# Moving the experts' up product from VectorE to ScalarE and GpSimd in a Mamba and mixture-of-experts kernel

## The reference, cut to what matters

```python
x = x + layernorm(mamba(layernorm(x)))        # x: 8 sequences x 1024 tokens x 256
x = x + layernorm(moe(layernorm(x)))

# inside mamba: 512 channels x 16 states
dA  = exp(dt[..., None] * A)
dBx = dt[..., None] * B[:, :, None, :] * xc[..., None]
h   = dA_t * h + dBx_t                        # a scan over the tokens
y_t = sum over states of h * C_t
y   = (y + xc * D) * silu(z) @ out_proj

# inside moe: 16 experts, 4 chosen per token, combine holds 0 for the others
g = einsum('th,eih->tei', x, gate_proj)
u = einsum('th,eih->tei', x, up_proj)
act = silu(g) * u
y = einsum('teh,te->th', einsum('tei,ehi->teh', act, down_proj), combine)
```

## Time and profile before

| what | value |
|---|---|
| median of 3 runs | 2711.35 us (2710.67 to 2711.61) |
| profiled execution | 2710.63 us, of which the span from first to last instruction 2708.8 us |
| VectorE busy | 2437.7 us, 90% of the span |
| TensorE busy | 2403.0 us, 89% |
| ScalarE busy | 1632.9 us, 60% |
| GpSimd busy | 1509.4 us, 56% |

### The profile page before, as it was taken

How to read it: one execution, slowest core, us unless ns; L and a number is a source line. 1 busy time by engine, 2 the same in 40 slices (tenths; PEclk the granted TensorE clock), 3 DMA queues, 4 the chain that set the end, 5 groups by cost and what they waited for, 6 DMA issues and landing times.

```text
span 2708.8 us, 27117 instructions
## 1 busy us (share of the span) xinstructions
PE 2403.0 (89%) x8416; PEld 1179.6 (44%) x8416; DVE 2437.7 (90%) x3236; ACT 1632.9 (60%) x3312; POOL 1509.4 (56%) x546
## 2 busy tenths in 40 slices
PE   5556898999989899998989999898999989898988
PEld 2112354544535454443545445353544535443554
DVE  3999999999999999999999999999999999999642
ACT  5566566566766656666665666666566666644331
POOL 0555555556665555665555566555656655565521
PEclk9778999999999999999999999999999999999999
DMA  4342434435353353535344353533535343352321
GB/s 157 139 146 81 156 109 133 158 115 163 120 161 110 130 163 115 163 120 158 113 131 163 100 177 120 161 110 127 167 109 169 120 154 109 127 163 84 86 59 60
DMA packets 174923, 352.38 MB, mean 130 GB/s; under 512 B 16283, under 2 KB 81596, under 8 KB 166332
## 3 DMA queue, kind: packets, MB, share of 16 engines
q1 hardware_dynamic: 164700, 334.93, 37.1%
q0 software_dynamic: 10080, 15.73, 3.6%
HBM read 291.35 MB, written 51.38 MB: 127 GB/s over the span
## 4 chain that ended last, share of the span: by engine, by line
DVE 59%; issue 18%; ACT 14%; PE 8%; DMA 1%; POOL 0%; DVEq 0%; SPq 0%; ACTq 0%; POOLq 0%
DVE hs L1019 27%; DVE hs L1005 13%; DVE th L1129 5%; DVE th L1134 5%; PE Gp L479 2%; ACT DX L604 2%; PE Up L487 2%; PE MY L497 2%; DVE XC L972 2%; ACT dA L586 1%; ACT L586 1%; ACT XC L657 1%; ACT SZ L662 1%; ACT my L765 1%; ACT DX L727 1%
## 5 line engine op out<-in xcount | busy, mean ns | idle before, releaser
L897 POOL TENSOR_TENSOR hs<-hs,Cb 128x2048 f32<-128x2048 f32 x256 | 1170.9, 4574 | 165.9 <-DVE hs L1005 165.9
L586 ACT ACTIVATE dA<-dtr,A 128x512 f32<-128x512 f32 x1024 | 701.8, 690 | 830.7 <-DVE hs L1019 829.7
L877 POOL TENSOR_TENSOR th<-th,cmb 128x512 f32<-128x512 f32 x256 | 338.2, 1326 | 818.1 <-DVE hs L1005 712.6
L1019 DVE TENSOR_TENSOR_SCAN hs<-dA,carry,hs 128x512 f32<-128x512 f32 x512 | 628.2, 1264 | 19.9 <-ACT dA L586 19.6
L1019 DVE TENSOR_TENSOR_SCAN hs<-dA,hs 128x512 f32<-128x512 f32 x512 | 595.9, 1203 | 30.7 <-ACT dA L586 30.2
L479 PE MATMUL Gp<-x2T,Wgu 128*128 128x512 f32 x1024 | 528.1, 640 | 106.1 <-DVE th L1129 105.9
L1005 DVE TENSOR_TENSOR hs<-dxr,Bb 128x2048 f32<-128x2048 f32 x256 | 602.7, 2354 | 7.7 <-DMA dxr<-dx_d 7.5
L487 PE MATMUL Up<-x2T,Wgu 128*128 128x512 f32 x1024 | 492.6, 604 | 0.0
L497 PE MATMUL MY<-Wdn,th 128*128 128x256 f32 x2048 | 485.7, 381 | 0.8 <-POOL th L877 0.8
L497 PEld LDWEIGHTS MY<-Wdn,th 128*128 128x128 f32 x2048 | 383.3, 190 | 136.7 <-issue 91.9
L479 PEld LDWEIGHTS Gp<-x2T,Wgu 128*128 128x128 f32 x1024 | 180.8, 195 | 439.1 <-issue 246.3
(11 more groups left out here) (165 smaller groups left out, 1860.5 us busy)
## 6 DMA issues: line engine op xcount, KB each, us to landing
dtr<-dt_d SPq DMA_DIRECT2D x64, 1024.0 KB, 5.6
dxr<-dx_d SPq DMA_DIRECT2D x128, 512.0 KB, 7.3
cmb<-cm_d SPq DMA_DIRECT2D x256, 256.0 KB, 3.7
Wdn<-in_w_dn SPq DMA_DIRECT2D x256, 128.0 KB, 3.6
Bb<-bc_d SPq DMA_DIRECT2D x64, 256.0 KB, 3.1
Cb<-bc_d SPq DMA_DIRECT2D x64, 256.0 KB, 4.1
dt_d<-XB SPq DMA_DIRECT2D x15, 1024.0 KB, 4.3
dx_d<-DX SPq DMA_DIRECT2D x15, 1024.0 KB, 5.9
```

The lines of the kernel that those rows point to most:

```text
L586: act.activation(dA[h % 2][:, :], dtr[:, M % 2, beta, :], ACT.Exp, scale=A[:, k:k + 1]).then_inc(s_dA, 1)
L877: pool.tensor_tensor(th[:, q % NTH, :], th[:, q % NTH, :], cmb[:, q % 2, :], ALU.mult).then_inc(m_a, 1)
L897: pool.tensor_tensor(hs[:, G % NH, :, :], hs[:, G % NH, :, :], Cb[:, s, :].unsqueeze(1).broadcast_to([P, NBETA, CH]), ALU.mult).then_inc(s ...
L1019: dve.tensor_tensor_scan(hv, dA[h % 2][:, :], hv, first, ALU.mult, ALU.add).then_inc(s_h, 1)
```

## The change

- ScalarE gets `keep_up`: it copies the up product from PSUM (Up) to a new SBUF buffer Ub. VectorE's `expert_up` is gone.
- GpSimd's `weigh` becomes two multiplications, Ub = Ub * cmb and th = th * Ub, and runs one group earlier (experts of G-1 in place of G-2).
- TensorE's up matmuls wait for `keep_up` in place of `expert_up`; `load_cm` waits for the first of the two multiplications two experts earlier.
- ScalarE's other work is moved between groups: the four z evictions and their fills (z0 to g = 4, z1 to g = 6 and 7, z2 and z3 to g = 9, ahead of the fill for dt), `p_x2` from the end of g = 6 to the middle of g = 7, `e_norm` from g = 7 to 8, `f_silu_z` from g = 12 to 10. `p_sums2` is removed: the mean of x1 is that of x, which is kept in x_nm.
- Some small buffers shrink or are shared (ln1, Ebias, z_s, to_y inside hs), and to_y comes by a DMA of its own.

```diff
-FILLS = ['b2', 'k2', 'r0', 'r1', 'b3', 'k3', 'z0', 'xp', 'x0', 'x1', 'rt', 'db', 'z1', 'ct', 'z2', 'z3', 'xT0', 'xT1', 'b0', 'b1']
+FILLS = ['b2', 'k2', 'r0', 'r1', 'b3', 'z0', 'k3', 'z1', 'xp', 'x0', 'x1', 'rt', 'z2', 'z3', 'db', 'ct', 'xT0', 'xT1', 'b0', 'b1']
...
+        Ub = sb('Ub', [P, CH])
...
                 if q % NE == 0:
                     sp.wait_ge(st_cm, 16 * (q // NE + 1))
                 if q >= 2:
-                    sp.wait_ge(m_a, q - 1)
+                    sp.wait_ge(m_w, q - 1)
                 sp.dma_start(cmb[:, q % 2, :], cm_d[q].partition_broadcast(P)).then_inc(ld_cm[q % 2], 16)
             def load_wd(q):
                 if q >= NWD:
...
             def up(q):
                 c, e = divmod(q, NE)
                 if q >= 1:
-                    pe.wait_ge(m_w, q)
+                    pe.wait_ge(m_us, q)
                 for k in range(KM):
                     mm = pe.matmul(Up[:, :], Wgu[:, k, e, DE:2 * DE], x2T[:, c % 2, k, :], start=k == 0, stop=k == KM - 1)
                 mm.then_inc(m_u, 1)
...
                 if now:
                     gate(now[0])
                     up(now[0])
-                if F and g in (0, 4, 6, 11):
-                    f_in(p, {0: 'b2', 4: 'b3', 6: 'z0', 11: 'z3'}[g])
+                if F and g in (0, 4, 6, 9):
+                    f_in(p, {0: 'b2', 4: 'b3', 6: 'z1', 9: 'z2'}[g])
                 if F and g in (1, 5):
                     f_conv(p, PE_CONV[g // 4])
                 if F and g == 7:
                     f_x(p)
-                if F and g == 9:
-                    f_dt(p)
                 if R_ and g in (2, 3):
                     p_out(p, g - 2)
                 if R_ and g == 8:
...
                     p_turn(p, 0)
                 if R_ and g == 8:
                     p_route(p)
-                if F and g in (9, 10):
-                    f_in(p, f'z{g - 8}')
+                if F and g == 4:
+                    f_in(p, 'z0')
+                if F and g == 9:
+                    f_in(p, 'z3')
+                    f_dt(p)
                 if in_e(p) and g == 13:
                     e_turn(p, 1)
                 if len(now) == 2:
...
                     act.wait_ge(m_d, q - NTH + 1)
                 act.activation(th[:, q % NTH, :], Gp[:, :], ACT.Tanh, scale=0.5).then_inc(m_th, 1)
 
-            def sums(x, s, to=None):
+            def keep_up(q):
+                act.wait_ge(m_u, q + 1)
+                if q >= 1:
+                    act.wait_ge(m_a, q)
+                act.activation(Ub[:, :], Up[:, :], ACT.Copy).then_inc(m_us, 1)
+
+            def sums(x, s):
                 for b in range(TB):
-                    ins = act.activation(to[b] if to else x[:, b, :], x[:, b, :], ACT.Copy, accum_out=s[:, 0, b:b + 1])
+                    ins = act.activation(x[:, b, :], x[:, b, :], ACT.Copy, accum_out=s[:, 0, b:b + 1])
                 return ins
 
-            def squares(x, s, steps, c, n, waste):
+            def squares(x, s, nm, waste):
+                for b in range(TB):
+                    ins = act.activation(waste[b], x[:, b, :], ACT.Square, bias=nm[:, b:b + 1], accum_out=s[:, 1, b:b + 1])
+                return ins
+
+            def means_squares(x, s, nm, steps, c, n, waste):
                 act.wait_ge(steps.sem, steps.at(c, n))
-                act.activation(s[:, 2, :], s[:, 0, :], ACT.Copy, scale=-1.0 / DM).then_inc(steps.sem, 1)
+                act.activation(nm, s[:, 0, :], ACT.Copy, scale=-1.0 / DM).then_inc(steps.sem, 1)
                 act.wait_ge(steps.sem, steps.at(c, n) + 1)
-                for b in range(TB):
-                    ins = act.activation(waste[b], x[:, b, :], ACT.Square, bias=s[:, 2, b:b + 1], accum_out=s[:, 1, b:b + 1])
-                return ins
+                return squares(x, s, nm, waste)
 
             dx_half = [flat[:, (TB + b) * DM:(TB + b + 1) * DM] for b in range(TB)]
             xb_half = [XB[:, b // 2, HIST + b % 2 * DM:HIST + (b % 2 + 1) * DM] for b in range(TB)]
...
 
             def p_squares(p):
                 act.wait_ge(e_act.sem, e_act.at(min(p + 2, NC - 1), 'sq'))
-                squares(rn, p_s, p_act, p - 1, 'rev1', dx_half).then_inc(p_act.sem, 1)
-
-            def p_sums2(p):
+                means_squares(rn, p_s, p_s[:, 2, :], p_act, p - 1, 'rev1', dx_half).then_inc(p_act.sem, 1)
+
+            def p_squares2(p):
                 if p < NC:
                     act.wait_ge(x1_sum, 16 * p)
                 else:
                     act.wait_ge(x1_last, 1)
-                sums(x1[:, (p - 1) % 2, :, :], b_s, dx_half).then_inc(p_act.sem, 1)
-
-            def p_squares2(p):
-                squares(x1[:, (p - 1) % 2, :, :], b_s, p_act, p - 1, 'sum2', dx_half).then_inc(p_act.sem, 1)
+                act.wait_ge(e_dve.sem, e_dve.at(p - 1, 'w1'))
+                squares(x1[:, (p - 1) % 2, :, :], b_s, x_nm[:, (p - 1) % 4, :], dx_half).then_inc(p_act.sem, 1)
 
             def p_ro(p):
                 c = p - 1
...
                     decay(G * NBETA + 3)
                 if len(experts_at(G - 1)) == 2:
                     tanh(experts_at(G - 1)[1])
+                    keep_up(experts_at(G - 1)[1])
                 if R_ and g in (3, 4):
                     p_rev(p, g - 3)
                 if R_ and g == 4:
...
                     p_x2T(p, 0)
                 if R_ and g == 9:
                     p_sig(p)
-                if F and g in (10, 11):
-                    f_z(p, g - 9)
+                if F and g == 7:
+                    f_z(p, 1)
+                if R_ and g == 7:
+                    p_x2(p)
                 if in_e(p) and g == 14:
                     e_xT(p, 1)
                 if g == 12 and 0 <= p - 2 < NC:
...
                     tanh(experts_at(G)[0])
                 if 0 <= p < NC and p % HALVES < HALVES - 1:
                     keep_ends(G)
+                if experts_at(G):
+                    keep_up(experts_at(G)[0])
                 if F and g in (0, 4):
                     f_b(p, 2 + g // 4)
                 if F and g in (1, 5):
...
                 if 0 <= p + 2 < NC and g == 3:
                     e_squares(p + 2)
                 if R_ and g == 5:
-                    p_sums2(p)
                     p_squares2(p)
                 if R_ and g == 4:
                     p_ro(p)
-                if F and g in (6, 11):
-                    f_z(p, {6: 0, 11: 3}[g])
+                if F and g == 4:
+                    f_z(p, 0)
                 if F and g == 6:
                     f_silu(p)
-                if R_ and g == 6:
-                    p_x2(p)
                 if F and g == 7:
                     f_xd(p)
-                if in_e(p) and g == 7:
-                    e_norm(p + 2)
                 if R_ and g == 8:
                     p_x2T(p, 1)
+                if in_e(p) and g == 8:
+                    e_norm(p + 2)
                 if F and g == 9:
+                    f_z(p, 2)
+                    f_z(p, 3)
                     f_softplus(p)
                 if R_ and g == 10:
                     p_cmT(p)
...
                     z_my(p - 2)
                 if g == 12 and 0 <= p - 2 < NC:
                     z_norm(p - 2)
-                if F and g == 12:
+                if F and g == 10:
                     f_silu_z(p)
                 if in_e(p) and g == 13:
                     e_xT(p, 0)
...
         def _(pool):
 
             def weigh(q):
+                pool.wait_ge(m_us, q + 1)
+                pool.wait_ge(ld_cm[q % 2], 16 * (q // 2 + 1))
+                pool.tensor_tensor(Ub[:, :], Ub[:, :], cmb[:, q % 2, :], ALU.mult).then_inc(m_w, 1)
                 pool.wait_ge(m_w, q + 1)
-                pool.wait_ge(ld_cm[q % 2], 16 * (q // 2 + 1))
-                pool.tensor_tensor(th[:, q % NTH, :], th[:, q % NTH, :], cmb[:, q % 2, :], ALU.mult).then_inc(m_a, 1)
+                pool.wait_ge(m_v, q + 1)
+                pool.tensor_tensor(th[:, q % NTH, :], th[:, q % NTH, :], Ub[:, :], ALU.mult).then_inc(m_a, 1)
 
             def add_x1(c):
                 pool.wait_ge(p_act.sem, p_act.at(c, 'ro'))
...
                     add_x1(p - 1)
                 if g == 13 and 0 <= p - 2 < NC - 1:
                     add_out(p - 2)
-                for q in experts_at(G - 2):
-                    weigh(q)
+                done = experts_at(G - 1)
+                if done:
+                    weigh(done[0])
                 if 0 <= G - 1 < NGRP:
                     read_out(G - 1)
+                if len(done) == 2:
+                    weigh(done[1])
 
         @block.vector
         def _(dve):
...
                 dve.wait_ge(m_th, q + 1)
                 dve.scalar_tensor_tensor(out=th[:, q % NTH, :], in0=th[:, q % NTH, :], scalar=1.0, in1=Gp[:, :], op0=ALU.add, op1=ALU.mult).then_inc(m_v, 1)
 
-            def expert_up(q):
-                dve.wait_ge(m_u, q + 1)
-                dve.wait_ge(m_v, q + 1)
```

(29 more changed lines are left out.)

31 lines of the change are left out of this document (14 added, 17 removed).

## The result

The changed kernel takes 3036.76 us (median of 4 runs, 3034.05 to 3041.56), the kernel before 2711.48 on the same chip. The ratio is 1.1201, 95% interval 1.1184 to 1.1217: 325 us slower. The forecast was 2957 us with a range of 2893 to 2995. The direction is as forecast, the size is 80 us beyond it and outside the range.

What follows compares the result with a forecast made beforehand. VectorE was taken as the bound, held by GpSimd through their shared port. 17.8 us a chunk gave 248 us over 223 groups; with -2 in the last chunk, 2710.6 became 2957 us, range 2893 to 2995.

Steps and rivals of the forecast that it cites:

- `inputs` is held until GpSimd ends: Plain group: VectorE's `inputs`, wanted at 5.17 us, waits for GpSimd's end at 7.29; period 9.37 us where it was 8.01.
- the third rival: Port holds but less time is added, as VectorE gets turns between GpSimd instructions: 2880 to 2920 us, chance 0.15.
- A chunk of +17.8 us: Steady chunk of 16 groups: 21.8 - 4.0 - 1.1 + 1.1 us, a period of about 176 in place of 158.
- The old waits: VectorE's existing waits for ScalarE, 5.1 us a chunk, in four or five groups, give back 4.0 us.
- `y_out` at g = 1 and 5: `y_out` reads PSUM and now lies beside `read_out`: saves 2 by 0.58, 1.1 us a chunk.
- The first expert's row: A chunk's first combine row, now needed one group later instead of two, makes GpSimd wait: adds 1.1 us a chunk.
- `load_cm` may go 1.28 us earlier than by the old wait and lies two groups ahead, so nothing behind it is later: SyncE's queue: the combine-row load's new place delays nothing behind it; no cost was added.
- the combine row ... 2 to 4 us a chunk more: Rival: port holds and lateness (combine row, DMAs, softplus or multiplication wait) comes on top: 2985 to 3020 us, chance 0.14.
- Groups 250 to 255 at 0: Two-expert groups: GpSimd needs 11.8 us, TensorE already makes them about 12 long, so 0 was added.
- The end at -2 and the start at 0: Last chunk loses the sums of x1 on its chain, -2 us; the start before group 27 has no experts, 0.
- ScalarE's moves at nothing: `keep_up` and the moved fills and evictions cost nothing, as ScalarE's cover grows; bound a few us a chunk.
- GpSimd doesn't pay: Where `inputs` overlaps `read_out` in groups 102 and 253, only VectorE is slowed; `read_out` took 4.83 and 5.03 us.

Runs made afterwards that it cites:

- isolated kernel: No part of the computation: VectorE and GpSimd run the same kinds of instructions alone and together; four VectorE multiplications take 8.90 us alone, 21.79 beside GpSimd's.
- 8-column kernels: Changed kernel with GpSimd's multiplications on 8 of 512 columns: both 2762.75 us, the first alone 2872.4 us; both, with early rows and read_out first at g = 11, 2674.82 us.
- kernel with early rows: Changed kernel with load_cm one group earlier in SyncE's queue, except for a chunk's first expert: 2979.26 us, ratio 1.0989 to the kernel before.

## Why the forecast had the direction and missed the size

**`inputs` is held until GpSimd ends: right.** The group is 9.34 us (9.37 forecast), GpSimd's end 7.26 us after the gate (7.29), the next gate 2.08 after that. The wait between the two multiplications, taken as 0.08 us between 0 and 0.16, is 0.08 (1148.72 less 1147.37 and 1.27). The isolated kernel shows the mechanism without the rest, and the 8-column kernels show that it is GpSimd's time that counts. In the isolated kernel VectorE does get a turn between two GpSimd instructions, as the third rival had it. Here it has none to use: `inputs` is ready 5.07 us after the gate, when `read_out`, GpSimd's last, has run since 2.72.

**A chunk of +17.8 us: right for what it counted.** With the rows early, groups 27 to 249 cost 246.4 us against 248, and a chunk +17.6. The places of a chunk, against before, give the terms one by one. Where none of the other terms applies (g = 0, 2, 3, 8, 9, 10, 14, 15) a group is 1.26 to 1.30 us longer, forecast 1.36. The old waits (g = 4, 6, 7, 12, 13) give back 3.7, forecast 4.0. `y_out` at g = 1 and 5 gives 0.8, forecast 1.1. The first expert's row costs 1.4 at g = 11, forecast 1.1. Every term is within 1.2 us a chunk, and they offset one another, so that the sum is right to 0.2 us is partly luck. VectorE's waits for ScalarE nearly went, as forecast.

**"`load_cm` may go 1.28 us earlier than by the old wait and lies two groups ahead, so nothing behind it is later": the step that failed.** It asked who stands behind the load. The cost was in who stands ahead of it. Until the change a row was mostly used two groups after its load was issued, and the margin covered whatever the queue did (in the steady chunks of before, 14 us or more from issue to use, but for the first expert's row); `weigh` then came a group sooner, and the margin fell to 6 to 9 us at the places where a store waits for ScalarE and 2 MB of dtr and dxr go first. Median landing times of 3.7 us said nothing of those places. The late rows cost 57.5 us. The forecast had seen the same for the first expert's row, at g = 11, and had priced that right; it didn't ask the question for the other fifteen. As a rival ("the combine row ... 2 to 4 us a chunk more") it had 0.14, with the size nearly right: 3.6 us a chunk; its times, 2985 to 3020, still end short of 3037. The forecast had also set a few us a chunk as the bound for what SyncE's and ScalarE's moves could cost, which holds 3.6 a chunk, and then took nothing; its range reaches 38 us above 2957, while 3.6 us a chunk are 50.

**Groups 250 to 255 at 0: mis-sized, 10.6 us.** The forecast set GpSimd's 11.8 us against "about 12" for TensorE. In the trace of before these groups take 10.5 us in the mean (52.3 for five); in the changed kernel 12.6. GpSimd's timeline of one of them in the kernel with early rows:

```profile
2752.18 4.51 POOL L916 TENSOR_TENSOR hs<-hs,Cb 128x2048 f32<-128x2048 f32 x1
2756.65 3.32 POOL L893 TENSOR_TENSOR Ub<-Ub,cmb 128x512 f32<-128x512 f32 x1
2760.05 1.26 POOL L896 TENSOR_TENSOR th<-th,Ub 128x512 f32<-128x512 f32 x1
2762.13 1.27 POOL L893 TENSOR_TENSOR Ub<-Ub,cmb 128x512 f32<-128x512 f32 x1 [0.82 <-issue]
```

From one `read_out` to the next are 12.53 us, 0.7 above the forecast's 11.8: the multiplication behind `read_out` is held by `inputs` in turn (3.32 us in place of 1.27, which stands for the 2.1 us of `inputs` itself), and 0.82 us go before the next one.

**The end at -2 and the start at 0: mis-sized, +17.3 and +3.0.** 10.5 of the 17.3 go when the loads are a group earlier. The experts' steady 5.16 us in the end is as before. What the other 6.8 (9.6 with `read_out` first at g = 11) and the 3.0 are made of stays open.

**ScalarE's moves at nothing: right to a few us in size, wrong in that their sign depends.** -9 us on the kernel before, +15 on the changed one, both within the "few us a chunk" that the forecast set as bound. The 15 are for the most part a share of the 57.5 for the rows: they lie at g = 9, where early rows give 16.68 us with the moves in place.

**"GpSimd doesn't pay": right for the two places it was read from, wrong as a rule.** In the kernel before, `read_out` is never longer than 5.06 us. Where `inputs` gets in first GpSimd pays too, as the last section shows. The sum didn't rest on it.

**What the page was to show.** L1023 was to have a median near 4.4 us. It is 4.34 in a plain group, but the median of all 256 is 2371 ns, because in 134 of them it is under 2.6 us: there another instruction of VectorE (a `conv`, a Newton step, routing) is the first behind GpSimd's and takes the waiting on itself (`conv` is at 1260 ns in the mean, 754 before), or `inputs` got in first; the mean of 3415 ns was the number to name. TensorE's waits for the gate are 15 us a chunk beside its weight loads' 24, where over 20 was said.

In sum: 248 forecast for the groups, 246.4 found once the rows are early; 57.5 for the rows; 10 for the two-expert groups; 11 for start and end. Together 325.

## What to carry to other kernels

Free time of an engine counts only if the trace shows it beside free operands: GpSimd's idle time in a plain group lay just where VectorE had two SBUF operands in hand, and 1.28 us of work put there cost 1.3 us a group. When a consumer is moved a step closer to its producer, list every DMA between them with what stands ahead of it in its queue at each place of the loop, and take the time at the worst place, not the median. And a kernel that leaves the suspected cost out (the 8 columns) should have the neighbouring costs taken out too, since a faster loop makes the next margin the bound.
